# Ends of two cross attentions in another order, the list of blocks in two parts, a bank freed earlier, semaphores cleared elsewhere: a two-layer decoder on one core

## The reference, cut to what matters

```python
x = x + _L0_attn_ref(_layernorm(x), ...)      # 16 heads of 16, window of 64 to either side
x = x + _L0_xattn_ref(_layernorm(x), ctx, ctx, ...)   # 16 heads of 16, 77 keys
x = x + _L0_ffn_ref(_layernorm(x), ...)       # 8 gated experts (silu), the best 2 per token
x = x + _L1_attn_ref(_layernorm(x), ...)      # 16 heads of 64, all 256 keys
x = x + _L1_xattn_ref(ctx, ctx, _layernorm(x), ...)   # 16 heads of 16, 77 keys
x = x + _L1_ffn_ref(_layernorm(x), ...)       # 8 plain experts (gelu), the best 2 per token
```

```python
attn = softmax(einsum('bhqd,bhkd->bhqk', q, k) / sqrt(16)); ctx = einsum('bhqk,bhkd->bhqd', attn, v)
top_v, top_i = jax.lax.top_k(einsum('bsd,ed->bse', x, Wg), 2)   # router
hidden = silu(h1) * h2; out = sum over the 2 experts of gating * (hidden @ W3[e])
```

## Time and profile before

| what | value |
|---|---|
| median of 3 runs | 1499.4 us (1499.39, 1499.4, 1502.16) |
| the profiled execution | 1493.69 us, span of its instructions 1492.0 us |
| mean granted clock of TensorE | 0.991 |
| PE busy | 1419.1 us, 95% of the span |
| PEld, DVE, ACT, POOL busy | 77%, 51%, 42%, 33% |
| transfers | 101.35 MB, mean 68 GB/s |

### The profile page before, as it was taken

How to read it: one execution, slowest core, us unless ns; L and a number is a source line. 1 busy time by engine, 2 the same in 40 slices (tenths; PEclk the granted TensorE clock), 3 DMA queues, 4 the chain that set the end, 5 groups by cost and what they waited for, 6 DMA issues and landing times. The chain is left out here.

```text
span 1492.0 us, 33834 instructions
## 1 busy us (share of the span) xinstructions
PE 1419.1 (95%) x11400; PEld 1146.9 (77%) x11401; DVE 754.9 (51%) x2161; ACT 625.6 (42%) x1726; POOL 493.2 (33%) x758
## 2 busy tenths in 40 slices
PE   7999989989999999999999999999899999999998
PEld 5666666667999999967777777777666679999997
DVE  6777757997333333344444444444378962222222
ACT  3444446653122222245454554554366543333332
POOL 3555532445212212223323322333124452222222
PEclk9999999999999999999999999999899989999999
DMA  9930000152243333210000000000001522534332
GB/s 319 343 107 25 23 16 16 44 178 80 37 147 93 91 88 95 37 53 1 1 1 1 1 1 1 0 1 1 1 16 45 186 76 36 148 93 96 94 90 34
DMA packets 84464, 101.35 MB, mean 68 GB/s; under 512 B 11483, under 2 KB 77379, under 8 KB 84355
## 3 DMA queue, kind: packets, MB, share of 16 engines
q1 hardware_dynamic: 64643, 77.58, 16.3%
q0 software_dynamic: 13680, 17.19, 6.7%
q10 hardware_dynamic: 6032, 5.12, 1.0%
HBM read 57.51 MB, written 39.59 MB: 65 GB/s over the span
## 5 line engine op out<-in xcount | busy, mean ns | idle before, releaser
L1784 POOL TENSOR_TENSOR L1a_prob<-L1a_prob,L1a_rtot 128x1024 f32<-128x1024 f32 x64 | 121.1, 1892 | 277.4 <-DVE L1a_rtot L1657 277.4
L2313 PEld LDWEIGHTS L0x_ps<-L0f_rows_t,L0f_w_up 128*128 128x128 f32 x1584 | 182.0, 192 | 10.4 <-issue 9.0
L2313 PE MATMUL L0x_ps<-L0f_rows_t,L0f_w_up 128*128 128x128 f32 x1584 | 184.2, 276 | 5.6 <-issue 4.8
L2389 ACT ACTIVATE L1f_hid<-L1x_ps,L1f_b_up 128x128 f32<-128x128 f32 x296 | 92.8, 364 | 164.2 <-PE L1x_ps L2313 163.8
L2313 PEld LDWEIGHTS L1x_ps<-L1f_rows_t,L1f_w_up 128*128 128x128 f32 x1184 | 140.2, 194 | 3.4 <-issue 1.6
L2313 PE MATMUL L1x_ps<-L1f_rows_t,L1f_w_up 128*128 128x128 f32 x1184 | 141.1, 278 | 0.6 <-ACT L1f_rows_t L2373 0.6
L2322 PE MATMUL L1x_ps<-L1f_w_down,L1f_hid 128*128 128x256 f32 x592 | 135.8, 383 | 1.9 <-DVE wv L2491 1.9
L2257 POOL TENSOR_TENSOR turn<-eps 128x1 f32<-128x1 f32 x74 | 13.6, 184 | 374.3 <-DVE wv L2491 370.7
L1726 ACT ACTIVATE L1a_prob<-L1a_ps_s,L1a_nmax 128x256 f32<-128x256 f32 x256 | 118.4, 474 | 38.5 <-DVE L1a_nmax L1652 38.5
L2322 PEld LDWEIGHTS L1x_ps<-L1f_w_down,L1f_hid 128*128 128x128 f32 x592 | 110.7, 192 | 16.0 <-issue 2.1
L1287 POOL TENSOR_SCALAR_AFFINE_SELECT L0a_prob<-L0a_prob 128x128 f32<-128x128 f32 (+1 forms) x256 | 82.4, 362 | 90.7 <-ACT L0a_prob L1219 90.7
(11 more groups left out here) (490 smaller groups left out, 2794.9 us busy)
## 6 DMA issues: line engine op xcount, KB each, us to landing
expert_table<-zero SPq DMA_DIRECT2D x1, 16640.0 KB, 69.7
L0f_w_up<-in_w_dram SPq DMA_DIRECT2D x8, 1408.0 KB, 6.4
L1f_w_up<-in_w_dram SPq DMA_DIRECT2D x8, 1024.0 KB
L1f_w_down<-in_w_dram SPq DMA_DIRECT2D x8, 1024.0 KB
L0f_w_down<-in_w_dram SPq DMA_DIRECT2D x8, 768.0 KB, 8.3
L1f_rows<-expert_table SPq DMA_DIRECT2D x35, 130.0 KB
L0f_rows<-expert_table SPq DMA_DIRECT2D x32, 130.0 KB
sums<-X SPq DMA_DIRECT2D x8, 256.0 KB, 2.5
```

The lines of the kernel that those rows point to most:

```text
L1784: eng.tensor_tensor(v, v, r.unsqueeze(2).to_broadcast([P, 2 * QT_N, S]), ALU.mult).then_inc(norm_done, 1)
L2313: ins = eng.matmul(ps_h[c][:, o:o + P], w_up[par][:, t, w0:w0 + P], rows_t[:, t, :], start=(t == 0), stop=(t == DT - 1))
L2389: ins = eng.activation(hid[:, c, k * P:(k + 1) * P], ps_h[c][:, k * P:(k + 1) * P], ACT.Gelu, bias=b_up[par][:, 2 * c + k:2 * c + k + 1])
```

## The change

- The copy of the queries is split: `mask_queries` is a function of its own. The bank is freed after the first copy. In unit 0, for queries that are among its helpers (L1x alone), the masking comes behind the four exponentials.
- In unit 14 PE runs `values(13)` ahead of the helpers, and DVE `sums(13)` right behind `shift(14)`, ahead of `slots(4)`. The snapshot behind slots(4) moves to unit 15, between `choose(5)` and `sums(14)`.
- Behind unit 15 PE makes `up(0, 0)` ahead of `values(15)`. ACT loads its table of functions behind `rows_out(0)` and not behind the last exponentials, and does `hidden(0, 0)` ahead of `route_norm(6)`.
- `last_at_least` (L0) moves from unit 10 to between the second and third hidden chunk of the first early block.
- The list of blocks is made in two parts: `count_blocks` at the old place, `list_blocks` behind the outputs of early block 1 and, in L0, the hidden values of early block 2.
- `turn_rows(0)` moves ahead of the down products of the last early block.
- After L0a and L1a semaphores are neither cleared nor is there a second barrier, and three idle products stand for eight behind the last projection. POOL clears those of L0a and L0x at the end of its list in L1a; those of L1a, L1x and the rest are cleared at the program's end.

```diff
--- before.py
+++ after.py
@@ -206,7 +206,13 @@
...
 
-    def take(eng, t, bank, values_free=None):
+    def mask_queries(eng, b):
+
+        for h in range(HALVES):
+            ins = eng.activation(q_m[b % 2][:, :, h, :], q_raw[b % 2][:, :, :], ACT.Identity, bias=none[:, 0:1], scale=half_mask[:, h:h + 1])
+            ins.then_inc(q_out, 1)
+
+    def take(eng, t, bank, values_free=None, masked_later=False):
         halves = bank.rearrange("p (c s) -> p c s", c=2)
...
@@ -232,10 +238,9 @@
...
             eng.wait_ge(q_out, 3 * b + 1)
-            for h in range(HALVES):
-                ins = eng.activation(q_m[b % 2][:, :, h, :], raw[:, :, :], ACT.Identity, bias=none[:, 0:1], scale=half_mask[:, h:h + 1])
-                ins.then_inc(q_out, 1)
             eng.sem_inc(out_scalar, 1)
+            if not masked_later:
+                mask_queries(eng, b)
             return
...
@@ -303,7 +308,7 @@
...
                 xn_done=xn_done, linked_v=linked_v, weights_in=weights_in, wait_out=wait_out, build=build,
-                statistics=statistics, take_keys=take_keys, take_bias=take_bias, norm=norm, take=take, clear=clear, spread=spread,
+                statistics=statistics, mask_queries=mask_queries, take_keys=take_keys, take_bias=take_bias, norm=norm, take=take, clear=clear, spread=spread,
                 spread_norm=spread_norm, make=make, sems=used)
...
@@ -563,30 +568,33 @@
...
                             first["statistics"](eng, b + 2)
+                        if u == units - 2:
+                            sums(u - 1)
                         if b >= 3:
...
                                 experts["order"](eng)
-                                if not final:
-                                    experts["last_at_least"](eng)
-                            for i, last in enumerate(FULL_BY):
-                                if b - 3 == last:
-                                    experts["snapshot"](eng, last)
+                            if b - 3 in FULL_BY and b < B - 1:
+                                experts["snapshot"](eng, b - 3)
                     else:
...
                         if u == units - 1:
+                            if b - 3 in FULL_BY:
+                                experts["snapshot"](eng, b - 3)
                             sums(u - 1)
...
                             add(b - 1)
-                    if u and u < units - 1:
+                    if u and u < units - 2:
                         sums(u - 1)
...
                 for c in range(experts["chunks"]):
+                    if c == 2 and not final:
+                        experts["last_at_least"](eng)
                     x["hidden"](0, c)
...
@@ -603,12 +611,14 @@
...
                 slots(B - 1)
-                route["list_blocks"](eng)
+                route["count_blocks"](eng)
                 x["token_and_gate"](1)
...
                         x["hidden"](n, c)
+                    if n == 2:
+                        route["list_blocks"](eng)
                     x["read_early"](n)
...
@@ -641,7 +651,7 @@
...
                         free = (values_done, CHUNKS * (t[1] - 1)) if t[0] == "v" and t[1] >= 2 else None
-                        first["take"](eng, t, src, free)
+                        first["take"](eng, t, src, free, t in LATE_MASKED)
                         return
...
@@ -668,6 +678,7 @@
...
                 x["start"]()
+                LATE_MASKED = [t for t in mid(0) if t[0] == "q"]
                 for t in REST:
...
@@ -678,8 +689,8 @@
...
                         exponential(u, r)
-                    if u == units - 1:
-                        x["table"]()
+                    for t in LATE_MASKED if u == 0 else []:
+                        first["mask_queries"](eng, t[1])
                     for t in of(END, u):
...
@@ -687,8 +698,9 @@
...
                 x["rows_out"](0)
+                x["table"]()
+                x["hidden"](0, 0)
                 route_norm(B - 2)
-                x["hidden"](0, 0)
                 x["hidden"](0, 1)
...
@@ -879,9 +891,11 @@
...
                         turn_tops(u)
+                    if u == units - 2:
+                        values(u - 1)
                     for t in mid(u):
                         make(t)
-                    if c == 0 and u:
+                    if c == 0 and 0 < u < units - 2:
                         values(u - 1)
...
@@ -891,10 +905,11 @@
...
                 x["turn"](0)
+                expert_bank_free(eng, "h", 0)
+                x["up"](0, 0)
                 values(units - 1)
-                for c in range(2):
-                    expert_bank_free(eng, "h", c)
-                    x["up"](0, c)
+                expert_bank_free(eng, "h", 1)
+                x["up"](0, 1)
                 make(("r0", B - 2))
...
@@ -919,14 +934,13 @@
...
                         x["turn"](n + 1)
+                    else:
+                        x["turn_rows"](0)
                     x["down"](n)
...
         held = used + first["sems"] + experts["sems"]
-        if not final:
-            return held
-        nc.clear_and_free_semaphores(held)
-        nc.all_engine_barrier(sem_only=True)
+        return held
 
...
@@ -1432,10 +1446,9 @@
...
                 make(B - 1, "o")
-                idle_products(eng, ps_o, ident, 8)
-
-        nc.clear_and_free_semaphores(used)
-        nc.all_engine_barrier()
+                idle_products(eng, ps_o, ident, 3)
+
+        return used
 
...
@@ -1798,6 +1811,8 @@
...
 
+                nc.clear_and_free_semaphores(held)
+
             @block.tensor
...
@@ -1921,10 +1936,9 @@
...
                 last_part(STEPS - 1)
-                idle_products(eng, ps_o, ident, 8)
-
-        nc.clear_and_free_semaphores(used + held)
-        nc.all_engine_barrier()
+                idle_products(eng, ps_o, ident, 3)
+
+        return used
 
...
@@ -2038,7 +2052,7 @@
...
 
-    def compute(eng):
+    def count_blocks(eng):
         early_experts = len(FULL_BY)
...
@@ -2061,6 +2075,7 @@
...
 
+    def list_blocks(eng):
 
...
@@ -2077,7 +2092,8 @@
...
 
-    route["list_blocks"] = compute
+    route["count_blocks"] = count_blocks
+    route["list_blocks"] = list_blocks
     return dict(blocks=blocks_i, base=base_i, list=list_i, expert=expert, expert_i=expert_i, left=by_place, full=full, order=order, snapshot=snapshot,
...
@@ -2352,11 +2368,10 @@
...
         def rest():
-            turn_rows(0)
             eng.wait_ge(listed["made"], 1)
...
 
-        return dict(start=start, turn=turn_early, up=up_early, down=down_early, rest=rest)
+        return dict(start=start, turn=turn_early, turn_rows=turn_rows, up=up_early, down=down_early, rest=rest)
 
...
@@ -2727,22 +2742,24 @@
...
                                   True, (ctx_landed, 16), [("x", 0), ("c", 0), ("c", 1), ("q", 0), ("c", 2), ("v", 0), ("k", 0, 0), ("k", 1, 0), ("b", 0), ("x", 1)])
-            attention_banded(nc, "L0a", env, 16 ** -0.5, wq0, wk0, wv0, wo0, bo0, ((x_first, 16), (x_second, 16), (x_rest, 16)),
+            of_first = attention_banded(nc, "L0a", env, 16 ** -0.5, wq0, wk0, wv0, wo0, bo0, ((x_first, 16), (x_second, 16), (x_rest, 16)),
                              (w0_landed, 32), (w0_rest, 48), prologue, later_loads, scale_bias, first)
...
             experts = moe(nc, inner, "L0f", env, True, weights, listed, route=routes[0], ahead=quads)
-            held = attention_crossed(nc, "L0x", env, wo1, bo1, first, routes[0], experts, False)
+            held = of_first + attention_crossed(nc, "L0x", env, wo1, bo1, first, routes[0], experts, False)
         with ExitStack() as inner:
...
                                   False, None, [("x", 0), ("k", 0, 0), ("k", 1, 0), ("q", 0), ("v", 0)], shared)
-            attention_quads(nc, "L1a", env, wq2, wk2, wv2, wo2, (gamma, beta), 1 / 8, ((w2_landed, 64), (ln_landed, 32)), x_back, quads, first, shared, other_tokens, held + quads["sems"])
+            of_second = quads["sems"] + attention_quads(nc, "L1a", env, wq2, wk2, wv2, wo2, (gamma, beta), 1 / 8, ((w2_landed, 64), (ln_landed, 32)), x_back, quads, first, shared, other_tokens, held)
             weights = expert_weights(nc, inner, "L1f", PLAIN_TILES * P, PLAIN_TILES, a["w1_1"], a["w2_1"], a["b1_1"], a["b2_1"])
...
             experts = moe(nc, inner, "L1f", env, False, weights, listed, route=routes[1])
-            attention_crossed(nc, "L1x", env, wo3, bo3, first, routes[1], experts, True)
+            held = of_second + attention_crossed(nc, "L1x", env, wo3, bo3, first, routes[1], experts, True)
+            nc.clear_and_free_semaphores(held)
+            nc.all_engine_barrier(sem_only=True)
 
...
 def kernel(**inputs):
```

## The result

The changed kernel took 1494.5 us, median of 8 runs (1490.8 to 1496.3), the kernel before 1500.8 over 8 runs beside it (1498.1 to 1508.6): a ratio of 0.9947, with a 95% interval of 0.9926 to 0.9968. The gain is 6 us by the medians and 8 by the ratio, where the prediction had 18.4. It was outside the range on the slow side. The profiled execution of the changed kernel took 1495.2 us, and by that profile the change gains nothing at all on the profiled 1493.7 of before.

The account below looks back on a forecast made before the run. The prediction took PE, the busiest engine, as the bound, improvable only in idle time and clock. Terms summed to 20.0, less 1.7 for one clock fall: 18.3 (18.4 with roundings), giving 1481.0 us, range 1474 to 1491.

Parts of the forecast that it names:

- the four scatters on POOL: At the ends of the cross attentions: pushed back 2.3 us with slots(4), costed at nothing; up to 2.3 per attention without cover.
- end of L0x: New order of last values, sums and first up products shortens PE's waits: 3.6 less 1.0, so 2.6 us gained.
- list L0: List in two parts and earlier turn of listed rows in L0: 1.5 + 0.8 - 0.4, so 1.9 us gained.
- join L1, and start of L1x: Shorter join, exponentials ahead of maskings and regained clock, less new waits: 5.9 us gained, 3.5 without any clock regained.
- end of L1x: New order brings the norm 1.5 us earlier; with 3.4 of clock, less about 0.9: 4.0 us gained.
- list L1: List in two parts in L1 removes output wait and clock loss, less 1.2 of waits for listed rows: 3.0 us gained.
- one more fall of the clock: Two new PE gaps were expected to bring one stretch at 1.2 GHz, taking 1.7 us off the gain.
- Both new gaps: New PE waits for norms in L1x, one at its start and one at its end, 1.85 us each.
- New waits take the place of the old at both ends: Rival: held sums, late slots(4) and scatters, late early rows cancel the ends' gains; 9.3 us gained, 1490, chance 0.08.
- All falls recur: Rival: every fall of the clock returns, shrinking both starts, L1x's end and the list; 13.5 us gained, 1486, chance 0.2.
- of seven such gaps four were followed by the lower level: PE gaps in the profile before: four of seven preceded 1.2 GHz, each costing 1.7 us or twice that.
- The stall weighed in the prediction: At attention ends, sums beside POOL's bias might stall like L524's comparisons: at most 2.1 us per attention, costed at nothing.

Follow-up runs that it names:

- e8: Changed kernel with the old order at both ends of the cross attentions: 1496.9 us, against 1493.1 for the changed kernel and 1496.6 before.
- e2: Changed kernel, unchanged, profiled a second time on the chip without held updates: 1473.0 us in one run, against 1493.9 before.
- e16: Changed kernel, unchanged, timed again on the chip without held updates: 1473.8 us over 6 runs, against 1490.1 before; ratio 0.9890.
- e12: Changed kernel with old list of blocks and old ends (joins, late maskings, last_at_least kept), updates held: 1495.1 us, against 1497.9 before; ratio 0.9982.
- e15: Changed kernel with scatters in pairs and the old one-piece list, no held updates: 1481.7 us, against 1476.4 with pairs alone and 1490.1 before.
- e1: Kernel before, unchanged, profiled a second time on the chip without held updates: 1491.2 us in one run, beside 1493.9.

## Why the prediction was wrong, point by point

**The step that failed** is the one that nobody wrote down as a step: every term of the sum lets a wait end when the producing instruction has ended. That was true of the profile that it was read from, which has no held update, and false on the chip of the comparison. The sum was then taken from the 1493.7 us of that profile and carried over to the comparison (1475.3 + 5.7 = 1481.0). The scatters have a part in one term by name: "the four scatters on POOL", pushed back with slots(4), were costed "at nothing", as GpSimd had time. The time was there (GpSimd's own idle time in that place of the first profile is 5.5 us, behind the bias; the 3.7 that the prediction gives is ScalarE's). That the push itself costs the gain is not borne out: e8, which undoes it with the rest of the order at the ends, is 3.8 us slower and not faster. What the scatters do to PE's updates beside them, at the old place and the new, was not in any row of before.

That this cost the gain is shown: on the chip without held updates the same kernel gained 16.3 us in timed runs (1490.1 to 1473.8) and 19.8 between the profiles (1493.7 to 1473.9), on the two with them 3.5 and 6.4; spacing the scatters gave 6.4 us back on one of these; and the kernel with pairs and spare additions took 1483.1 us without held updates and 1484.7 with them. A part of the loss goes by the clock: the mean granted clock is 0.991 in the first profile of the changed kernel and 0.998 in that of e2, which is some 10 of the 22 us between them (an estimate from these two shares of the span). The first profile of before has 0.991 too, so between these two profiles next to nothing came of what the forecast took from the clock.

**The terms without held updates.** The profile of e16 beside that of before, by the starts of the same matmuls (what PE has gained at the first of L0x's scores, its last scores, the last r0, the second block, and so on):

| term | forecast | measured |
|---|---|---|
| join L0 | 1.6 | 2.1 |
| `last_at_least` | 1.3 | 1.3 |
| end of L0x | 2.6 | 2.1 |
| list L0 | 1.9 | 1.9 |
| L0f to the start of L1a | 0 | -0.2 |
| join L1, and start of L1x | 5.9 | 2.3 + 3.4 |
| end of L1x | 4.0 | 4.2 |
| list L1 | 3.0 | 3.5 |
| rest of L1f | 0 | -0.3 |
| clear at the end | -0.3 | -0.5 |
| one more fall of the clock | -1.7 | 0 |
| sum | 18.4 | 19.8 |

No term is off by more than 0.5 us but the last. These are differences of two executions; by the medians of timed runs the gain on that chip is 16.3 us, with an interval from 12.5 to 20.4 by the ratio. Both new gaps are there, 1.6 us (forecast 1.85) and 1.3 (L637 in L1x), and neither was followed by the lower clock: in the stretches that answer to the earlier trace rows it is 1.00 throughout. PE's waits and these windows in e16:

```profile
PE L1x_ps L816 <- ACT L1x_xr L637: 1.6, 2, 1.3
...
PE L1x_ps L298 <- ACT L1x_xn L205: 1.6, 1, 1.6
```
```profile
1057.00:1065.00 8.00, 5.74 (x64) 4.01 (x64) 4.54 (x8) 1.84 (x4) 2.34 (x5) 1.00 0.00 0
1065.00:1075.00 10.00, 8.34 (x103) 5.74 (x104) 4.68 (x5) 7.54 (x15) 1.67 (x4) 1.00 0.01 2
1178.00:1188.00 10.00, 7.98 (x99) 5.71 (x92) 8.12 (x26) 6.58 (x14) 6.06 (x9) 1.00 0.30 97
1205.00:1213.00 8.00, 8.00 (x59) 7.59 (x58) 5.87 (x27) 2.78 (x9) 5.88 (x6) 1.00 0.31 90
```

**Where it went with them.** The profile of the first comparison lags that of e2 by 2.3 us from unit 14 of L0x on (the scores above), by 4.3 at r0(6) (counts and routed rows held, so that the first up products wait 1.8 us and not 0.7), by 6.4 at r0(7) (logits held, ScalarE 2.4 late), by 7.8 after a fall of the clock at 358.6, by 10.1 after the third hidden chunk. In L1x it is 12.4 from unit 14 on, 16.0 at r0(6), with 10 us at half clock, 17.1 at r0(7), 19.5 at the second block, and 22.4 at the end, 1.7 of it by one more fall of the clock at 1297. So 10 us in L0 and 12 in L1, nearly all behind held updates or falls of the clock near them. Not all: the fall at 1297 follows a wait of 1.96 us for the transfer of listed rows, with no held update beside it. That the new order makes the holds dear, as in the old one PE had slack, its own waits for sums, at just these places, is my reading and not shown part by part: the list loses its 5 us, the ends by e8 only 1 to 3 of 6.6, and e12 lacks some 6 us in the parts that are neither.

**The rivals.** "New waits take the place of the old at both ends (held sums, slots(4) and its scatters late ...)", 1490 with a chance of 0.08, came nearest in place and in size; its mechanism was not there. "All falls recur" (1486, with 0.2) was 8 us off, but right on the clock, which is 0.991 in both first profiles; it had no room for the held updates. That the changed order is more open to disturbance than the old was not among the cases, and the range, taken from terms that all stood on one undisturbed profile, was too narrow for that. There was a sign: the profiled execution of before was 5.7 us faster than its median. I carried this over as a constant, without asking what made the other runs slower (whether held updates did can't be told, as they have no trace here). And one count was wrong: "of seven such gaps four were followed by the lower level" leaves out two waits of PE of the same length in that profile, 1.6 us at the end of L0x (L865, behind L483) and 1.7 in L1a (L300), so it is four of nine.

**The stall weighed in the prediction.** VectorE's comparisons L524 were costed at nothing for the sums beside the bias, though they could have cost 4.1 us. In e16 it can be seen: at the end of L1x the reciprocal of sums(14), from 1179.77, takes 1.76 us with GpSimd's bias beside it from 1180.97, and as much at 1172.04, where no bias runs; the addition behind it takes 0.68. The two L524 (L529 there), now away from the bias, take 0.26 us in place of 2.07. So the sums have no such stall, and the rule cited there (the Trainium skill, SBUF — State Buffer, on the shared port pair) agrees with that.

## What to carry to other kernels

Before summing differences from one profile, ask how it stands to the median, and look for "remote" waits and late updates in a second one, from another chip if there is one: an order that removes slack can pay in full for a disturbance that the old order absorbed. Where GpSimd issues scatters in rows of four or more, put other work of a microsecond or more between pairs of them, or move them away from the places where another engine waits for PE. A change that gains 5.4 us on one chip and nothing that can be told on another, as the list in two parts does, should be timed on both before it is kept: where updates are held, pairs (1485.2 and, with the old list, 1483.9) beat both kernels; where they are not, the changed kernel as it is (1473.8) beats pairs by 2.5.

## What the runs showed of the hardware

- On three of four chips, and in the first comparison's profile of the changed kernel, PE's semaphore updates came up to 3.8 us late beside GpSimd's scatters; on one chip never, in eight profiles at two times. The scatters took as long on both kinds, 0.96 us in the median. Profiles with held updates also have fewer records of semaphore updates (10786 to 11129 against 11915 to 11979).
- At unit 14 the last timely update came 1.4 us after the start of the first of four scatters (315.33), the first held one was due at 1.8 (315.76) and came at 317.54, and three later ones were posted together 1.0 us after the end of the last scatter. With pairs no update in the units was more than 1.3 us late by the start of the engine that waited. What inside the chip holds the updates is open: no run here shows it. Whether the updates of VectorE and ScalarE are held too is open as well, since records of theirs are missing at these places.
- The clock: in e15 not one stretch at 1.2 GHz lies before the last 10 us, in e16 one of 3.4 us at 657.8. Gaps of PE of 1.3 and 1.6 us in L1x were not followed by one; in the first profile of before, of nine gaps of 1.5 to 2.2 us behind the start, four were. It is not the same from one execution to the next: e1, the same kernel without held updates, has the same nine gaps, and a fall followed three of them, one of which (1.6 us at 342.2) had none in the first profile. Falls also came with no gap over 1.3 us in the 10 us before, at 335.0 in e1 and 657.8 in e16.
